# One two-part product for the bias rows, fewer waits and a new order of steps in a two-layer recurrent and attention kernel

## Chip, cores, metric

The kernel runs on one core of a Trainium2 chip. The metric is the device time of one execution in microseconds (us), the median of several runs. The core has five engines with an instruction stream each: PE (TensorE, matrix products), ACT (ScalarE), DVE (VectorE), POOL (GpSimd) and SP (here only the issuer of DMA transfers). Each works through its stream in order; they meet at semaphores.

## What is computed

Two layers on an input of 2 sequences x 2048 tokens x 256 features. In each layer a block's output is multiplied by the SiLU of a second block and added to the input. Cut to what matters here:

```python
# layer 0: a Mamba block, then a gelu MLP; gate: a gated MLP in blockwise FP4
def step(h, inp):
    dt_t, B_t, C_t, x_t = inp
    dA = jnp.exp(dt_t[..., None] * A)          # A: 512 channels x 16 states
    h = dA * h + dt_t[..., None] * B_t[:, None, :] * x_t[..., None]
    y = jnp.sum(h * C_t[:, None, :], axis=-1)
h = jax.nn.silu(fp4_linear(x, w_gate)) * fp4_linear(x, w_up)   # 704 wide
# layer 1: 16-head attention over the 2 sequences; gate: three blocks of
y = _layernorm(_qlora_linear(h, ...)); y = jax.nn.gelu(y); h = _qlora_linear(y, ...) + h
x = x + s * jax.nn.silu(g)
```

The first linear of each of the three blocks, the q and v parts of the attention's input and its output projection have a bias vector of 256 features. Those six are the "bias rows" below.

## The kernel before

**Tiling.** Time is cut into 16 chunks of 128 positions of both sequences (256 tokens, `TOK`). Weights are prepared once (lines 205 to 399: FP4 rounding, transposes, folding of the low-rank parts). Then the five engines run one pipelined loop over `PERIODS` (lines 1276 to 1321).

**The order is written by hand.** Each engine has a list of words, its plan (lines 74 to 106); in a period it runs every word once. A `+` behind a word means the chunk one later than the period's, a `-` one earlier, so one period mixes stages of up to five chunks. A word is a step of `pe_step`, `act_step`, `pool_step`, `dve_step` or `sp_step`, which waits for the semaphores that it needs and then issues its instructions.

**The state engine.** The recurrence runs for 16 states n, each in two halves a and b of the channels. Per state:
- `drive n` (POOL, lines 960 to 972) multiplies `wx` by the state's row of B, then adds eight start values in a second small instruction;
- `exp n` (ACT, line 742) writes the decay into one of three PSUM buffers `unit`, two instructions a half;
- `scan n` (DVE, line 1127) runs the recurrence of a half, `hc n` (line 1133) multiplies it by the row of C, `clr n` (line 1140) clears column 0 of the unit;
- `out n` (ACT, line 750) saves the last column as `carry`. Half k of the chunk uses unit k mod 3, so `exp` of a half waits for the `out` of the half three before it, and that `out` waits for its `clr`;
- `sum n` (PE, line 537) adds it into `y_ps` by transposes; `rows n` (SP) fetches B and C rows from DRAM.

Around it: `dt` and `wx` (DVE) make the chunk's step sizes and `wx`; `log` (POOL) and `dtexp`, `dtln` (ACT) come before `dt`; `arg` (POOL), `first` (ACT) and `fix0`, `fix1` (POOL) make the start values; `yg` (DVE) reads `y_ps` after `sum15`; `fin` (POOL, lines 1068 and 1072) is the last step of a chunk, two tensor operations.

**The banks of PE.** All other products go into three PSUM banks in turn, in the order of `PE_PLAN` without the `sum`s and `skip` (lines 122 to 124). A product waits until the one three places before it has been read by its consumer; `USE` (line 48) names who that is:

```python
BANK = {_key: _k % NBANK for _k, _key in enumerate(ORDER)}
EARLIER = {_key: ORDER[_k - NBANK] for _k, _key in enumerate(ORDER) if _k >= NBANK}
```

The gated MLP is `g00 g01 g10 g11` and `u00 u01 u10 u11` (line 593; first digit: sequence, second: half of the 704 columns). ACT applies SiLU to each g (line 827); DVE's `ug0` multiplies first u00, then u01 into it (two instructions of line 1183), `ug1` does u10 and u11. A g's bank is free after its SiLU, a u's after its multiplication in `ug`. `scale0`, `j0in`, `round0`, `j0out` quantize the product. A bias row is a product (lines 515 to 518) of a one-hot column of `ident` with `b_rows`, in float32.

Of the kernel before, what the change touches and what calls it, by code (L numbers as in the profile page):

```python
# [36 lines left out]
XW = NTAP - 1 + TC  # L37
MAGIC = 1.5 * 2 ** 22
# [42 lines left out]
    exp12a- hq1- hq2- out11a- exp12b- out11b- h1-- exp13a- ctx-- out12a- out12b- exp13b- out13a- exp14a- exp14b-  # L81
    usave dtln gatec--- out13b- exp15a- out14a- exp15b- first out14b- exp0a b1n-- gatem- b1g-- out15a- exp0b
    out15b- s1-- yg0- xq exp1a out0a out0b exp1b yg1- exp2a out1a exp2b g00 out1b g01 exp3a out2a exp3b g10
    out2b g11 exp4a out3a opn- out3b exp4b xn+ xhf+ u2- h2-- exp5a out4a exp5b f10- f11- out4b f12- exp6a out5a
# [11 lines left out]
    hc2a scan2b clr2a hc2b op- clr2b scan3a scan3b h2-- hc3a hc3b clr3a clr3b ug0 scan4a scale0 ug1 hc4a scan4b
    clr4a hc4b scan5a clr4b scan5b hc5a xscale+ hc5b clr5a clr5b round0 scan6a b2s-- hc6a scale1 scan6b clr6a
    hc6b scan7a hc7a clr6b scan7b clr7a hc7b clr7b x1- scan8a conv0+ scan8b hc8a hc8b clr8a conv1+ round1 b0s-
    clr8b scan9a scan9b hc9a hc9b clr9a clr9b scan10a hc10a scan10b clr10a scan11a score- scan11b hc10b hc11a
    clr10b hc11b clr11a attn- clr11b h1- scan12a hc12a scan12b hc12b clr12a clr12b scan13a hc13a clr13a f++  # L100
# [1247 lines left out]
```

## Time and profile before

| | |
|---|---|
| median of 3 runs | 1848.96 us (1847.87 to 1852.0) |
| the profiled execution | 1856.52 us, its span 1854.7 us |
| granted clock of TensorE, mean | 0.953 |
| instructions | 28175 |
| ACT table loads | 109 before `exp` alone, 1283 ns each |
| loop | 16 chunks; first `scan` at 184.5 us, last at 1752.1 us |

The span is the time between the first and the last instruction of the profiled execution; 1.8 us lie outside it. "Busy" is the time in which an engine worked on something; idle time is laid to the engine whose signal ended it. Idle time on an engine that isn't the bottleneck costs nothing. Line numbers stand as L965.

### The profile page before, as it was taken

The numbers are of one execution on the slowest core, as the hardware profiler recorded it, in microseconds if no ns is written. First come the engines' busy times: TensorE is split into PE (matmuls) and PEld (weight loads), VectorE is DVE, ScalarE is ACT, GpSimd is POOL, SyncE is SP. The second block draws the span as 40 slices with busy tenths as digits, with TensorE's granted clock in tenths as the row PEclk, the third lists the DMA queues.
The fourth block names the chain that finished last, engine by engine and source line by source line (L and its number), as shares of the span: only waits on it lengthen the run. The fifth ranks groups of instructions, "written<-read, shape, count | busy, mean of one in ns | idle before, by whom it ended". The sixth has DMA issues, their size and how long they took to land.

```text
span 1854.7 us, 28175 instructions
## 1 busy us (share of the span) xinstructions
PE 1577.4 (85%) x7632; PEld 1164.4 (63%) x7632; DVE 1551.4 (84%) x2882; ACT 1437.5 (78%) x3076; POOL 1252.4 (68%) x1313
## 2 busy tenths in 40 slices
PE   0083768899999999999989999999989999999875
PEld 0051556586767677776767676767667767767653
DVE  0623999999999999999999999999999999999811
ACT  0034678898989898989889888989888989888723
POOL 0304676777777786868687777778686868787522
PEclk9976789999999999999999999999999999999987
DMA  8000111111111111111111111111111211111100
GB/s 209 0 6 29 52 47 58 47 57 37 58 48 60 43 52 51 59 47 52 52 52 52 44 51 50 58 47 46 58 52 47 63 41 58 46 44 55 35 0 12
DMA packets 68395, 91.70 MB, mean 49 GB/s; under 512 B 15674, under 2 KB 34686, under 8 KB 68238
## 3 DMA queue, kind: packets, MB, share of 16 engines
q1 hardware_dynamic: 68238, 89.91, 15.8%
q8 instruction: 62, 1.02, 0.2%
q14 instruction: 95, 0.78, 0.1%
HBM read 85.17 MB, written 4.72 MB: 48 GB/s over the span
## 4 chain that ended last, share of the span: by engine, by line
PE 27%; POOL 20%; DVE 16%; issue 16%; ACT 12%; POOLq 0%; ACTq 0%; DVEq 0%; DMA 0%
PE bank L511 10%; POOL drive L965 10%; PE bank L627 6%; DVE unit L1127 4%; DVE hc L1133 3%; PE bank L516 2%; PE y_ps L537 2%; ACT unit L742 2%; PE bank L498 1%; PE bank L563 1%; ACT op_a L709 1%; DVE xc L1158 1%; ACT L709 1%; ACT L923 1%; POOL s L1068 1%
## 5 line engine op out<-in xcount | busy, mean ns | idle before, releaser
L965 POOL TENSOR_TENSOR drive<-wx,rows 128x1024 f32<-128x1024 f32 x256 | 604.1, 2360 | 163.3 <-DVE unit L1127 82.8
L1127 DVE TENSOR_TENSOR_SCAN unit<-unit,drive 128x512 f32<-128x512 f32 x512 | 616.7, 1221 | 30.7 <-POOL drive L971 23.4
L742 ACT ACTIVATE unit<-dt,aneg 128x254 f32<-128x254 f32 x1024 | 441.9, 468 | 19.8 <-ACT carry L750 0.7
L1133 DVE TENSOR_TENSOR hc<-unit,rows 128x512 f32<-128x512 f32 x512 | 340.9, 684 | 8.8 <-issue 3.0
L537 PE MATMUL y_ps<-ident,hc 128*128 128x128 f32 x2048 | 278.1, 282 | 52.5 <-DVE hc L1133 52.4
L537 PEld LDWEIGHTS y_ps<-ident,hc 128*128 128x128 f32 x2048 | 241.2, 145 | 115.3 <-DVE hc L1133 71.8
L742 ACT ACT_TABLE_LOAD x109 | 139.8, 1283 | 3.7
L750 ACT ACTIVATE carry<-unit 128x4 f32<-128x4 f32 x512 | 79.3, 169 | 66.8 <-DVE unit L1140 63.0
L627 PE MATMUL bank<-op_a,w_f 128*128 128x256 f32 x512 | 115.7, 385 | 11.2 <-ACT op_a L709 11.2
L709 ACT ACT_TABLE_LOAD x77 | 98.8, 1283 | 22.4 <-PE bank L498 21.6
L511 PE MATMUL bank<-w_f,wide 128*128 128x256 f32 x512 | 113.3, 379 | 1.5 <-ACT wide L709 1.5
L627 PEld LDWEIGHTS bank<-op_a,w_f 128*128 128x128 f32 x512 | 97.0, 192 | 27.1 <-ACT op_a L709 11.9
L511 PE MATMUL bank<-w_d,hq_t 128*128 128x256 f32 (+1 forms) x384 | 109.3, 436 | 0.0
L511 PEld LDWEIGHTS bank<-w_f,wide 128*128 128x128 f32 x512 | 96.0, 190 | 14.9 <-ACT wide L709 1.7
L516 PE MATMUL bank<-b_rows,ident 6*128 6x512 f32 (+1 forms) x192 | 100.9, 605 | 0.0
L511 PEld LDWEIGHTS bank<-w_d,hq_t 128*128 128x128 f32 (+1 forms) x384 | 78.6, 219 | 27.0 <-issue 16.4
L593 PE MATMUL bank<-w_g,xq_t 128*128 128x352 f32 x256 | 87.3, 464 | 5.0 <-ACT xq_t L821 5.0
L1013 POOL TENSOR_SCALAR wide<-wx 128x1024 f32<-128x1024 f32 x16 | 58.4, 3652 | 46.8 <-ACT wx L813 46.8
L384 PE MATMUL bank<-ident,gate_raw 88*128 88x88 f32 x32 | 4.9, 355 | 97.2 <-POOL down_raw L314 97.2
L593 PE MATMUL bank<-w_u,xq_t 128*128 128x352 f32 x256 | 84.0, 460 | 1.3 <-ACT hq L827 1.1
L1038 POOL TENSOR_TENSOR hq<-q,j_scl 128x704 f32<-128x704 f32 x32 | 44.4, 1387 | 54.1 <-DVE q L1114 54.1
L722 ACT ACTIVATE xht<-bank,b_sm 128x256 f32<-128x256 f32 x96 | 48.7, 558 | 38.2 <-POOL b_sm L953 38.2
(220 smaller groups left out, 3439.4 us busy)
## 6 DMA issues: line engine op xcount, KB each, us to landing
rows<-rows_scratch SPq DMA_DIRECT2D x256, 256.0 KB, 3.3
x_t<-in_L_attn_x_dram SPq DMA_DIRECT2D x16, 256.0 KB, 3.7
x<-in_L_attn_x_dram SPq DMA_DIRECT2D x16, 256.0 KB, 3.3
out_dram<-x SPq DMA_DIRECT2D x16, 256.0 KB, 2.1
w_f<-in_L_attn_ffn_w_dram SPq DMA_DIRECT2D x2, 1024.0 KB
q_raw<-in_L_ffn_qweights_dram SPq DMA_DIRECT2D x1, 1536.0 KB
w_in<-in_L_attn_in_proj_w_dram SPq DMA_DIRECT2D x1, 1024.0 KB
qkv_raw<-attn_in_proj_weight_dram SPq DMA_DIRECT2D x1, 768.0 KB
```

Source lines behind the costliest of these rows:

```text
L511: last = t.matmul(dst[:, j * D:(j + 1) * D], lhs(k, j), rhs(k), start=(k == 0 and j == 0), stop=(stop and k == kp - 1), skip_group_check=True)
L516: return t.matmul(dst[:, 0:wide_ * D], ident[0:NROW, row:row + 1].to_broadcast([NROW, P]), b_rows[:, None, :].to_broadcast([NROW, wide_, D ...
L537: last = t.matmul(y_ps[j][:, g * P:(g + 1) * P], hc[n % NPROD][:, g * B + j, :], ident[:, :], start=False, stop=(n == NS - 1), is_transpos ...
L593: last = t.matmul(dst[:, 0:IH], xq_t[:, k, j, :], wt[:, k, half * IH:(half + 1) * IH], start=(k == 0), stop=(k == KD - 1))
L627: last = t.matmul(dst[:, a * TOK:(a + 1) * TOK], w_f1[:, k, (2 * m + a) * P:(2 * m + a + 1) * P], op_a[:, k, :], start=(k == 0 and a == 0) ...
L709: last = a_.activation(dst(k), src[:, k * TOK:(k + 1) * TOK], func, scale=scale(k), bias=bias(k))
L742: last = a_.activation(u[:, k * TOK:(k + 1) * TOK].rearrange("p (b t) -> p b t", b=B)[:, :, 1:TC], dt[p][:, g, :].rearrange("p (b t) -> p ...
L750: a_.activation(carry[:, n, 4 * half:4 * half + 4], unit_of(ch, n, half)[:, :].rearrange("p (s t) -> p s t", t=TC)[:, :, TC - 1], ACT.Copy)\
L965: g_.tensor_tensor(drive[n % 2][:, :, :].rearrange("p (g b) t -> p g b t", b=B), wx[p][:, :, :].rearrange("p g (b t) -> p g b t", b=B), ro ...
L1013: g_.tensor_scalar(tmp_u, wx[p][:, :, :], 1.0, -1.0, ALU.add, ALU.add).then_inc(S["sp_pool"], 1)
L1127: v.tensor_tensor_scan(u[:, :], u[:, :], d, 0.0, ALU.mult, ALU.add).then_inc(S["scan_done"], 1)
L1133: v.tensor_tensor(hc[n % NPROD][:, 4 * half:4 * half + 4, :].rearrange("p (g b) t -> p g b t", b=B), unit_of(ch, n, half)[:, :].rearrange( ...
```

## The change

1. **Bias rows.** `b_two` (64 rows of 256, type F32R) holds the bias vectors rounded to F32R in rows 0 to 5 and what the rounding left in rows 32 to 37; one product with the two-hot column `pick` adds both. It takes the place of the float32 product. Four more small loads, one POOL memset and five small DVE operations are added in the preparation.
2. **Waits.** In `exp`, `out`, `drive`, `scan` and `hc`, waits that an earlier wait of the same engine already implies are issued only where they are new.
3. **Order.** All five plans are replaced. Each holds the same words as before.

```diff
 PE_PLAN = """
-    b0a-- xp kv-- sum8- dt0 hqT0- q-- b0T-- sum9- v1-- dt1 b0b-- sum10- hqT1- hqT2- sum11- ctxT-- h1T-- b2b---
-    b1a-- sum12- sum13- dn- sum14- b1T-- sum15- ao-- xqT ygT0- skip ygT1- g00 sum0 g01 op- g10 sum1 g11 b1b--
-    u00 u01 sum2 u10 u2T- u11 sum3 h2T-- f10- f11- f12- f13- b2a-- uT+ sum4 sum5 f2- b2T-- xi0+ xi1+ sum6 z0+
-    sum7 xn1T- xi2+ xi3+ z1+
+    z1 b0a-- sum8- xp kv-- dt0 q-- b0T-- sum9- dt1 hqT0- sum10- v1-- b0b-- sum11- hqT1- h1T-- ctxT-- hqT2-
+    sum12- b1a-- dn- sum13- b2b--- sum14- b1T-- xqT sum15- ao-- ygT0- ygT1- skip sum0 g00 op- b1b-- g01 u00 g10
+    h2T-- g11 u01 sum1 sum2 u2T- u10 u11 f10- sum3 sum4 f11- f12- f13- sum5 b2a-- uT+ f2- b2T-- xi0+ xi1+ sum6
+    z0+ xn1T- xi2+ xi3+ sum7
 """
 ACT_PLAN = """
...
+    exp10b- b0n-- out9b- out10a- exp11a- exp11b- kv-- dt0 out10b- b0g-- aexp-- dt1 v1-- dtexp exp12a- out11a-
+    hq0- exp12b- out11b- exp13a- hq1- h1-- out12a- ctx-- out12b- exp13b- exp14a- dtln out13a- hq2- out13b-
+    exp14b- out14a- exp15a- exp15b- out14b- exp0a b1n-- first gatem- gatec--- b1g-- xq out15a- exp0b out15b-
+    exp1a s1-- out0a yg0- usave out0b yg1- exp1b exp2a out1a exp2b g00 out1b g01 out2a opn- g10 h2-- g11 exp3a
+    out2b exp3b exp4a out3a u2- exp4b out3b xn+ exp5a out4a xhf+ exp5b out4b exp6a f10- f11- f12- out5a out5b
+    f13- exp6b exp7a out6a u+ out6b exp7b out7a b2n-- exp8a exp8b b2g-- tap0+ tap1+ hn- z0+ out7b xn1- tap2+
+    tap3+ xc0+ out8a z1+ xc1+ exp9a exp9b out8b exp10a out9a xp+
 """
 POOL_PLAN = """
-    drive14- drive15- b1-- arg fix0 drive0 xout fin--- drive1 drive2 hb1-- drive3 fix1 f+ drive4 op- drive5 j0in
...
+    drive14- drive15- b1-- arg xout fix0 drive0 fin--- drive1 hb1-- drive2 drive3 op- drive4 f+ drive5 fix1
+    drive6 s0b- drive7 j0in drive8 hb2-- b2-- j0out j1in x1- drive9 hb0- diff- drive10 j1out b0- xin+ drive11
+    drive12 drive13 log+
 """
 DVE_PLAN = """
-    clr15a- xround yg- scan0a clr15b- hc0a scan0b clr0a hc0b clr0b scan1a hc1a clr1a scan1b scan2a hc1b clr1b
...
+    hc15b- wx clr15a- yg- scan0a clr15b- hc0a scan0b clr0a hc0b clr0b scan1a scan1b hc1a clr1a hc1b op- clr1b
+    scan2a hc2a h2-- clr2a scan2b hc2b clr2b ug0 scan3a hc3a scan3b clr3a hc3b clr3b scan4a hc4a scale0 clr4a
+    scan4b scan5a hc4b ug1 clr4b xscale+ scan5b scan6a hc5a clr5a hc5b hc6a clr5b clr6a round0 scan6b hc6b
+    scan7a clr6b b2s-- scan7b hc7a clr7a scale1 hc7b x1- conv0+ scan8a clr7b scan8b hc8a hc8b clr8a clr8b conv1+
+    round1 b0s- scan9a scan9b hc9a scan10a clr9a hc9b scan10b hc10a clr9b clr10a hc10b clr10b scan11a f++ score-
+    scan11b hc11a hc11b clr11a clr11b attn- scan12a h1- scan12b hc12a scan13a clr12a hc12b clr12b hc13a clr13a
+    b1s- scan13b hc13b clr13b scan14a hc14a scan14b clr14a hc14b scan15a dt+ clr14b xround+ hc15a scan15b
 """
...
             def bias_row(dst, row, wide_):
-                return t.matmul(dst[:, 0:wide_ * D], ident[0:NROW, row:row + 1].to_broadcast([NROW, P]),
-                                b_rows[:, None, :].to_broadcast([NROW, wide_, D]), start=False, stop=True,
+                return t.matmul(dst[:, 0:wide_ * D], pick[:, row:row + 1].to_broadcast([2 * LOW, P]),
+                                b_two[:, None, :].to_broadcast([2 * LOW, wide_, D]), start=False, stop=True,
                                 skip_group_check=True)
...
                 u = unit_of(ch, n, half)
-                act.wait_ge(*at("dt_ready", ch))
+                if (n, half) == (0, 0):
+                    act.wait_ge(*at("dt_ready", ch))
...
-                act.wait_ge(*at("carry_in", ch, 1 + n // 8))
+                if n % 8 == 0 and half == 0:
+                    act.wait_ge(*at("carry_in", ch, 1 + n // 8))
...
-                dve.wait_ge(*at("drive_ready", ch, 2 * n + 2))
+                if half == 0:
+                    dve.wait_ge(*at("drive_ready", ch, 2 * n + 2))
...
-                dve.wait_ge(*(at("y_summed", ch, n + 2 - NPROD) if n >= NPROD else at("y_summed", ch - 1, NS + n + 2 - NPROD)))
-                dve.wait_ge(*rows_in(ch, n))
+                if half == 0:
+                    dve.wait_ge(*(at("y_summed", ch, n + 2 - NPROD) if n >= NPROD
+                                  else at("y_summed", ch - 1, NS + n + 2 - NPROD)))
```

The `drive` step's waits for `wx_ready` and `carry_in` are cut in the same way.

## Rows read from the trace of the kernel before

**Rows 1.** The page, part 1: busy time, share of the span, instructions
```profile
PE 1577.4 (85%) x7632; PEld 1164.4 (63%) x7632; DVE 1551.4 (84%) x2882; ACT 1437.5 (78%) x3076; POOL 1252.4 (68%) x1313
```
**Rows 2.** Busy time in one period: start:end, length, busy by engine, granted clock
```profile
863.87:963.53 99.66, 93.36 (x468) 68.95 (x468) 93.98 (x179) 88.89 (x191) 76.86 (x82) 1.00 0.16 52
1063.45:1163.12 99.67, 94.79 (x470) 70.34 (x468) 93.99 (x179) 88.90 (x191) 76.83 (x82) 0.98 0.17 51
```
**Rows 3.** Waits of DVE from 900 to 999.64: total us, times, longest
```profile
DVE unit L1127 <- POOL drive L971: 1.7, 2, 1.3
DVE prod L1224 <- PE bank L516: 0.7, 1, 0.7
DVE s L1205 <- PE bank L529: 0.5, 1, 0.5
DVE xc L1158 <- ACT xc L776: 0.4, 1, 0.4
DVE hc L1133 <- issue: 0.2, 1, 0.2
```
**Rows 4.** Timeline of DVE: start us, us long, instruction, [idle before]
```profile
947.80 0.13 DVE L1140 MEMSET unit<- 128x4 f32 x2
960.09 1.21 DVE L1170 TENSOR_TENSOR wx<-dt,xc 128x1024 f32<-128x1024 f32 x1
965.89 1.28 DVE L1195 TENSOR_TENSOR sz<-y_ps,sz 128x512 f32<-128x512 f32 x2
967.09 1.22 DVE L1127 TENSOR_TENSOR_SCAN unit<-unit,drive 128x512 f32<-128x512 f32 x1
972.32 1.23 DVE L1127 TENSOR_TENSOR_SCAN unit<-unit,drive 128x512 f32<-128x512 f32 x1 [1.29 <-POOL drive L971]
985.84 0.95 DVE L1183 TENSOR_TENSOR hq<-hq,bank 128x352 f32<-128x352 f32 x2
```
**Rows 5.** Timeline of POOL
```profile
943.02 3.65 POOL L1013 TENSOR_SCALAR wide<-wx 128x1024 f32<-128x1024 f32 x1 [1.77 <-ACT wx L813]
961.43 2.35 POOL L965 TENSOR_TENSOR drive<-wx,rows 128x1024 f32<-128x1024 f32 x1
963.86 0.27 POOL L971 TENSOR_TENSOR drive<-drive,fix 128x8 f32<-128x8 f32 x1
967.07 1.26 POOL L1068 TENSOR_TENSOR s<-s,gate_c_sb 128x512 f32<-128x512 f32 x1
989.68 1.39 POOL L1030 TENSOR_TENSOR q<-hq,j_rcp 128x704 f32<-128x704 f32 x1 [0.57 <-DVE j_rcp L202]
```
**Rows 6.** Timeline of PE
```profile
900.89 1.12 PE L516 MATMUL bank<-b_rows,ident 6*128 6x512 f32 x2
919.44 1.15 PE L563 MATMUL bank<-u_t,w_in 128*128 128x262 f32 x4 [0.15 <-ACT sz L788]
983.24 2.53 PE L593 MATMUL bank<-w_u,xq_t 128*128 128x352 f32 x8
```
**Rows 7.** Timeline of ACT
```profile
947.90 0.24 ACT L750 ACTIVATE carry<-unit 128x4 f32<-128x4 f32 x2 [0.31 <-DVE unit L1140]
948.44 0.87 ACT L742 ACTIVATE unit<-dt,aneg 128x254 f32<-128x254 f32 x2 [0.30 <-ACT carry L750]
977.56 0.46 ACT L827 ACTIVATE hq<-bank 128x352 f32<-128x352 f32 x1
978.04 1.28 ACT L742 ACT_TABLE_LOAD   x1
```
**Rows 8.** Waits over the whole span, in the preparation
```profile
DVE q_amax L196 <- DMA lb_raw<-in_L_ffn_lora_b_dram: 45.3, 1, 45.3
DVE unit L1316 <- PEq L287: 34.4, 1, 34.4
```
**Rows 9.** Waits of DVE for ACT over the whole span
```profile
DVE unit L1127 <- ACT unit L742: 4.6, 8, 1.3
```
**Rows 10.** The page, part 6: DMA issues, KB each, us to landing
```profile
rows<-rows_scratch SPq DMA_DIRECT2D x256, 256.0 KB, 3.3
```

More of the change, by code:

```diff
@@ L37 @@
 XW = NTAP - 1 + TC
+LOW = 32
 MAGIC = 1.5 * 2 ** 22
@@ L79 @@
+    h2T-- g11 u01 sum1 sum2 u2T- u10 u11 f10- sum3 sum4 f11- f12- f13- sum5 b2a-- uT+ f2- b2T-- xi0+ xi1+ sum6
+    z0+ xn1T- xi2+ xi3+ sum7
 """
 ACT_PLAN = """
[L81 to L84, printed above, removed]
@@ L85 @@
-    f13- exp6b out5b u+ exp7a b2n-- out6a exp7b out6b exp8a out7a exp8b b2g-- tap0+ tap1+ hn- z0+ xn1- tap2+
-    tap3+ z1+ out7b out8a xc0+ xc1+ exp9a exp9b out8b exp10a b0n- kv- xp+ out9a out9b exp10b exp11a dt0+ out10a
-    exp11b hq0 b0g- aexp- dt1+ out10b v1- dtexp+
+    exp10b- b0n-- out9b- out10a- exp11a- exp11b- kv-- dt0 out10b- b0g-- aexp-- dt1 v1-- dtexp exp12a- out11a-
+    hq0- exp12b- out11b- exp13a- hq1- h1-- out12a- ctx-- out12b- exp13b- exp14a- dtln out13a- hq2- out13b-
+    exp14b- out14a- exp15a- exp15b- out14b- exp0a b1n-- first gatem- gatec--- b1g-- xq out15a- exp0b out15b-
@@ L96 @@
[L96 to L100, printed above, removed]
@@ L102 @@
+    round1 b0s- scan9a scan9b hc9a scan10a clr9a hc9b scan10b hc10a clr9b clr10a hc10b clr10b scan11a f++ score-
+    scan11b hc11a hc11b clr11a clr11b attn- scan12a h1- scan12b hc12a scan13a clr12a hc12b clr12b hc13a clr13a
+    b1s- scan13b hc13b clr13b scan14a hc14a scan14b clr14a hc14b scan15a dt+ clr14b xround+ hc15a scan15b
 """
 SP_PLAN = """
-    rows8- rows11- load+ rows10- rows12- rows13- wr rows14- rows15- rows0 rows1 rows3 rows2 store--- rows4
-    again- rows6 rows5 rows9 rows7
+    rows15-- rows14-- rows0- rows1- rows2- rows3- rows5- rows4- store---- rows7- rows6- rows8- rows10- rows9-
@@ L106 @@
+    again-- rows12- rows11- load+ rows13- wr
 """
@@ L168, in program @@
         w_l = sb("w_l", [P, NLIN, KD, D])
-        b_rows = sb("b_rows", [NROW, D])
+        b_rows = sb("b_rows", [2 * LOW, D])
+        b_two = sb("b_two", [2 * LOW, D], F32R)
+        pick = sb("pick", [2 * LOW, LOW], F32R)
         b_f2 = sb("b_f2", [P, D])
@@ L227, in program @@
                 (w_f2[:, :, :], ffn_w2.rearrange("(k p) n -> p k n", p=P)),
-                (b_rows[0:3, :], biases.rearrange("(i k) d -> i k d", k=2)[:, 0, :]),
-                (b_rows[3:4, :].rearrange("o (h d) -> o h d", d=HD),
-                 qkv_b.rearrange("(h c d) -> c h d", c=3, d=HD)[0:1, :, :]),
-                (b_rows[4:5, :].rearrange("o (h d) -> o h d", d=HD),
-                 qkv_b.rearrange("(h c d) -> c h d", c=3, d=HD)[2:3, :, :]),
-                (b_rows[5:6, :], ao_b[None, :]),
+                *[piece for r in (0, LOW) for piece in (
+                    (b_rows[r:r + 3, :], biases.rearrange("(i k) d -> i k d", k=2)[:, 0, :]),
+                    (b_rows[r + 3:r + 4, :].rearrange("o (h d) -> o h d", d=HD),
+                     qkv_b.rearrange("(h c d) -> c h d", c=3, d=HD)[0:1, :, :]),
+                    (b_rows[r + 4:r + 5, :].rearrange("o (h d) -> o h d", d=HD),
+                     qkv_b.rearrange("(h c d) -> c h d", c=3, d=HD)[2:3, :, :]),
+                    (b_rows[r + 5:r + 6, :], ao_b[None, :]))],
                 (b_l[:, :, :], biases.rearrange("(i k) d -> i k d", k=2)[None, :, 1, :].to_broadcast([P, 3, D])),
@@ L353, in _ @@
                     dve.wait_ge(c_done, 5)
+                    v.tensor_copy(pick[0:LOW, :], ident[0:LOW, 0:LOW]).then_inc(c_prep, 1)
+                    v.tensor_copy(pick[LOW:2 * LOW, :], ident[LOW:2 * LOW, LOW:2 * LOW]).then_inc(c_prep, 1)
+                    dve.wait_ge(c_done, 6)
+                    for r in (0, LOW):
+                        v.tensor_copy(b_two[r:r + NROW, :], b_rows[r:r + NROW, :]).then_inc(c_prep, 1)
+                    dve.wait_ge(c_prep, 6 * len(quants) + 7)
+                    v.tensor_tensor(b_two[LOW:LOW + NROW, :], b_rows[LOW:LOW + NROW, :],
+                                    b_two[LOW:LOW + NROW, :].bitcast(F32), ALU.subtract).then_inc(c_prep, 1)
                     for g in range(DG):
@@ L962, in pool_step @@
                 pool.wait_ge(*rows_in(ch, n))
-                pool.wait_ge(*at("wx_ready", ch))
+                if n == 0:
+                    pool.wait_ge(*at("wx_ready", ch))
                 pool.wait_ge(*at("scan_done", ch, 2 * n - 2))
@@ L969, in pool_step @@
                 pool.wait_ge(*at("drive_ready", ch, 2 * n + 1))
-                pool.wait_ge(*at("carry_in", ch, 1 + n // 8))
+                if n % 8 == 0:
+                    pool.wait_ge(*at("carry_in", ch, 1 + n // 8))
                 g_.tensor_tensor(drive[n % 2][:, :, 0], drive[n % 2][:, :, 0], fix[:, n, :], ALU.add)\
@@ L1296, in _ @@
             def _(act):
-                act.wait_ge(c_done, 7)
-                act.wait_ge(c_prep, 6 * 3 + 3 + DG + NUNIT)
+                act.wait_ge(c_done, 8)
+                act.wait_ge(c_prep, 6 * 3 + 3 + 5 + DG + NUNIT)
                 for c in PERIODS:
@@ L1305, in _ @@
             def _(pe):
-                pe.wait_ge(c_done, 7)
+                pe.wait_ge(c_done, 8)
                 for c in PERIODS:
```

8 lines of the change are left out of this document (3 added, 5 removed).

## The prediction

> **What bounds it now.** I read the shares of busy time first [rows 1]: PE 85% and DVE 84% of the span, but that mixes preparation and loop. So I cut out single periods of the loop by the busy time in windows [rows 2]. One lasts 99.66 us, and in it DVE works 94.0, PE 93.4 to 94.8, ACT 88.9 and POOL 76.9 us. DVE and PE are both nearly full. Then I listed what DVE waits for in one period [rows 3]: 1.7 + 0.7 + 0.5 + 0.4 + 0.2 = 3.5 us. The other 2.1 us of its idle time are gaps of some 30 ns between dependent instructions. So DVE alone would need 99.66 - 3.5 = 96.2 us a period even if nobody ever kept it waiting. That is the floor. The change takes no instruction from DVE in the loop, so it can win at most 3.5 us a period, and it loses whatever new waits its order puts on DVE. All the rest of my work is this count of waits on DVE.
>
> **The bias rows.** There are six a chunk, five of 512 columns and one of 256. One of 512 columns is now two passes over the array that take 1.05 us (1.12 with the tail) [rows 6]. The new one is one instruction. No row shows an F32R product. Its bounds are half of the present pair (0.53 us, if only one of two instructions goes) and a quarter (0.26, if the remaining one also streams twice as fast). I take 0.3. PE gains 5.5 x 0.75 = 4.1 us a period (bounds 2.9 and 4.4). The Trainium skill (FP8 and Floating Point Precision, TensorE Precision Notes) says that true FP32 takes four passes through the array; by it a single pass would be the quarter, 0.26 us; no row here shows a single pass. PE thus needs about 90 of 99.66 us. That relieves it, but DVE's 96.2 stays.
>
> **The waits left out.** On DVE 64 waits a period go (16 before scans, 48 before `hc`), on ACT 61, on POOL about 30. A wait is handled ahead while the engine still works on the instruction before: only 0.2 us a period of DVE's idle time is put down to issue [rows 3]. I take 0.2 us a period; the upper bound is the 2.1 us of small gaps, which I don't believe because the dependent ones remain. A cost below nothing has no reason.
>
> **Table loads on ACT.** Walking the old list I count 19 changes between Exp, Ln, Silu, Gelu and tanh-Gelu a period, in the new one 14. Each costs 1.28 us [rows 7], so ACT gains 6.4 us. The Trainium skill (ScalarE: Activation LUTs, What ACT_TABLE_LOAD costs) puts a load at about 2.7 us, which would make it 13.5 us; the trace has less than half of that. ACT isn't the bound, so this is worth something only where DVE waits for ACT.
>
> **The order.** I walked DVE's new list and asked at each step who releases it, and how much DVE work lies between the releasing and the released step. Five places come out short by construction, wherever the rest of the pipeline stands:
> 1. `wx` to `scan0a`. `drive0` needs `wx`. From the start of `wx` at 960.09 to the end of drive's second instruction at 963.86 + 0.27 is 4.04 us [rows 4, 5], 4.1 with the signal. Before, `scan15b`, two `hc`, `xround` and `yg` lie between. Now only `wx` (1.21, of which the next instruction overlaps 0.09), `clr15a` and `yg` (1.28, likewise) do: 2.4 us. New wait: 1.7.
> 2. `scan1a`. POOL still has `fin` (2 x 1.27) between `drive0` and `drive1` (2.35 + 0.3, as `drive0` [rows 5]): `scan1a` can't start before 5.3 us after `scan0a`, and DVE has 3.9 us of work. This is the 1.29 us of today [rows 4], and stays: 1.3. `xout` moved ahead of `drive0` changes nothing here.
> 3. `ug0`. In the new PE order (`u00 g10 h2T g11 u01`) g11 stands three places behind u00 and takes its bank, and u01 comes after g11. So g11 can't start until `ug0` has multiplied u00, and `ug0`'s second instruction can't start until g11 and then u01 are done. That such bank waits bind is to be seen where xi3 waits for the SiLU of z0, three places before it [rows 6]. Two such products back to back take 2.53 us [rows 6]. With the first multiplication (0.51) and two signals of 0.1 the second starts 3.2 us after the first, against 0.44 now (0.95 for both) [rows 4]. New wait: 2.7. DVE takes its list in order, so nothing fills it.
> 4. `scan3a`. ACT has `g11 exp3a` in this order. From g11's start: product 1.3, SiLU 0.46, table load 1.28, `exp` 0.87 [rows 7] and signals 0.2 make 4.1 us; `ug0` would let DVE go at 2.6 + 0.45 = 3.05. New wait: 1.0.
> 5. `scan10b`. It needs `clr9a`, `out9a`, `exp10b`. From the end of the clears (947.80 + 0.13) to the end of `exp` (948.44 + 0.87) today's fastest case takes 1.4 us [rows 4, 7]; `xp+` (0.3) now sits between. DVE has only `hc9b` (0.7) there. New wait: 0.8 to 1.0; I take 0.8. In the old list every such pair has at least 1.8 us of DVE work between.
>
> Sum: 1.7 + 1.3 + 2.7 + 1.0 + 0.8 = 7.5 us a period, 96.2 - 0.2 + 7.5 = **103.5 us**.
>
> Four more places are short if the other engines stand where I place them when I lay the lists side by side from these durations:
> - `op` on DVE: PE gets to `sum0` before `hc0b` is done and holds g00 and `op` behind it, 0.9 us;
> - `round0`: `j0in` (1.39 [rows 5]) now stands behind `drive7`, which waits for `scan5b`, 1.1 us;
> - `conv0`, now ahead of `scan8a`: ACT puts `exp8b`, a table load and `b2g` before `tap0`, 1.6 us;
> - `scan14a`: `log` (3.65 [rows 5] and two operations of drive's size) still precedes `drive14`; 0.4 to 0.6 us as now.
>
> They add up to 4.2 us, more than half of which hangs on where PE stands, and today's waits for PE at L1224 and L1205 are of the same kind. A wait in one place gives the next engine time to catch up, so I take half: 2.1. The period becomes 105.6 us, bounds 103.5 and 107.7.
>
> SP's list now fetches the rows in swapped pairs (`rows15` before `rows14`, `rows5` before `rows4` and so on). The even one of a pair thus waits for one state's `hc` more, and lands 3.3 us after its issue [rows 10]. The tightest is `drive4`: `rows4` is released by `hc1b` and can be there some 5 us later, when POOL has just done `drive3` and the four small operations of `op`. POOL is idle 22.8 us a period [rows 2], so I take nothing; if that cover is gone, about 1 us, within the bounds.
>
> **Outside the loop.** The four added loads come before the wait of 45.3 us for the last load, a few tenths to 2 us; the five DVE operations lie in a stretch in which DVE afterwards idles 34.4 us [rows 8], nothing. The last chunk has the new waits too, but no full DVE. I take +1.
>
> **Sum.** The loop has 15 full periods. 15 x (105.6 - 99.66) = 89, with +1 it is 90 us: 1856.5 + 90 = 1946.5 for an execution like the profiled one. That one was 7.6 us above the median of the runs shown, so the forecast is **1939 us**. With the bounds 103.5 and 107.7 it is 1908 and 1971; this case's own range is 1905 to 1985.
>
> **Rivals.**
> - *Milder.* The five places are real but shorter, for instance because DVE's 2.1 us of small gaps shrink with its waits and signals are quicker than I took them: a period of 101 to 103.3, 1869 to 1904 us, slower still. For it: the signal times are my estimates. Against: items 2 and 3 rest on measured durations alone.
> - *Faster.* The one mechanism is PE relief without the ring at `ug0` and the early `scan0a`: should my reading of the bank rotation be off, so that u01 is in its bank when `ug0` starts, and `yg` be long enough for `drive0`, then PE's 4.1 us and ACT's 6.4 us remove the waits of today save `scan1a`: 96.2 + 1.3 = 97.5, 15 x -2.2 = -32, 1817 us. It decides from less than 3.3 us of waits left on DVE a period. For it: PE and ACT do get slack, and four of the five waits of today come from them or are near. Against: rows and code of items 1 and 3.
> - *No change.* New waits of just about 3.5 us: 1845 to 1853.
> - *Worse.* PE, held at g11 and at `sum4`, falls behind in the second half and `q`, `b0a` come late: over 108 us a period, above 1985.
> - *The bias product doesn't get shorter.* Then PE needs 94 of 105.6 us; nothing changes in the time, and it is no case of its own.
>
> **Chances.** Forecast 0.68, milder 0.12, worse 0.05, faster 0.12, no change 0.03. The range must leave out no more than 2 in 10: forecast and milder together are 0.80, 1865 to 1985. A measurement of this kernel tells a difference from about 0.2%. Slower by more than that: 0.68 + 0.12 + 0.05 = 0.85; within: 0.03; faster: 0.12.
>
> **What would show it.** In the trace of the changed kernel: in each period a wait of 2.7 us of DVE L1183 for PE L593; `scan0a` and `scan1a` waiting 1.7 and 1.3 us for POOL L971; waits of DVE L1127 for ACT L742 of about 1 us twice a period (4.6 us in the whole span now [rows 9] would become over 25); 14 table loads a period; PE busy about 90 us a period; a period of 104 to 107 us. Wrong if L1183 never waits, or if DVE's busy time itself changed. If the five waits are there and the period is still under 101 us, my floor is wrong.

## The result, and the profile after

| | before | changed |
|---|---|---|
| median, 4 runs each | 1849.46 us (1847.87 to 1852.0) | 2082.4 us (2081.7 to 2089.97) |
| ratio, with its 95% interval | 1 | 1.1267 (1.1238 to 1.1297) |
| profiled execution, its span | 1856.52, 1854.7 us | 2089.97, 2088.2 us |
| period of the loop, mean of ten | 99.72 us | 115.42 us |
| DVE kept waiting, per period | 3.55 us | 16.73 us |
| granted clock of TensorE, mean | 0.953 | 0.927 |

The change costs 233 us. The forecast was 1939 us with a range of 1865 to 1985: the sign was right and the size was not, by 143 us. Fifteen periods of 115.4 instead of the forecast 105.6 us make 147, about as much, so the error lies in the loop.

In the changed kernel the numbers of the lines are some 13 to 19 higher: scan is L1145, hc L1152, clr L1159, out L765, exp L756, drive L981 and L988, ug L1202, the bias product L529.

The page of the changed kernel, part 1 (to hold against [rows 1]) and two lines of part 5 (costliest groups; busy us, mean ns of one, idle before it and its releaser):

```profile
PE 1606.4 (77%) x7536; PEld 1190.0 (57%) x7536; DVE 1583.3 (76%) x2887; ACT 1339.3 (64%) x2999; POOL 1228.7 (59%) x1314
...
L1145 DVE TENSOR_TENSOR_SCAN unit<-unit,drive 128x512 f32<-128x512 f32 x512 | 618.7, 1222 | 112.1 <-ACT unit L756 69.0
...
L765 ACT ACTIVATE carry<-unit 128x4 f32<-128x4 f32 x512 | 85.5, 172 | 375.9 <-DVE unit L1159 374.7
```

All shares fell. DVE's busy time rose by 32 us, with five more instructions, and PE's rose by 29 us although 96 instructions are gone. The scan waits for 112 us in the whole span, and 69.0 of them end at an `exp` of ACT, where it was 4.6 [rows 9].

Next, one period: its length, busy time by engine (PE, PEld, DVE, ACT, POOL), granted clock. It answers to [rows 2]:

```profile
999.66:1115.15 115.49, 96.34 (x465) 71.31 (x464) 96.12 (x179) 82.68 (x185) 75.15 (x82) 0.96 0.14 44
```

DVE executes the same 179 instructions in 96.1 us that took it 94.0. Then the waits of DVE in the same period (total us, times, longest), which answer to [rows 3]:

```profile
DVE unit L1145 <- ACT unit L756: 4.0, 6, 1.0
DVE hq L1202 <- PE bank L606: 2.7, 1, 2.7
DVE unit L1145 <- POOL drive L988: 2.7, 2, 1.5
DVE b_st L1100 <- PE bank L529: 2.4, 1, 2.4
DVE prod L1243 <- PE bank L529: 2.0, 1, 2.0
DVE q L1124 <- POOL q L1047: 1.0, 1, 1.0
DVE sd L1252 <- ACT sd L938: 0.9, 1, 0.9
DVE s L1218 <- PE bank L524: 0.8, 1, 0.8
DVE xc L1177 <- ACT xc L791: 0.4, 1, 0.4
...
```

To see which step each of them is, I went down DVE's timeline of that period with the new list beside it (start, us, instruction, in brackets the wait; the instructions between these are left out):

```profile
1000.37 0.84 DVE L201 TENSOR_SCALAR x_scl<-x_amax 128x32 f32<-128x32 f32 x1
...
1007.11 0.53 DVE L1124 TENSOR_SCALAR q<-q 128x704 int32<-128x704 int32 x1 [1.00 <-POOL q L1047]
...
1046.94 0.69 DVE L1243 TENSOR_TENSOR prod<-bank,kv 128x512 f32<-128x512 f32 x1 [1.98 <-PE bank L529]
1055.54 1.23 DVE L1145 TENSOR_TENSOR_SCAN unit<-unit,drive 128x512 f32<-128x512 f32 x1 [1.01 <-ACT unit L756]
1064.15 0.76 DVE L1100 BATCH_NORM_STATS2 b_st<-bank 128x6 f32<-128x256 f32 x2 [2.39 <-PE bank L529]
1083.25 1.23 DVE L1145 TENSOR_TENSOR_SCAN unit<-unit,drive 128x512 f32<-128x512 f32 x1 [1.47 <-POOL drive L988]
1088.42 2.35 DVE L1145 TENSOR_TENSOR_SCAN unit<-unit,drive 128x512 f32<-128x512 f32 x2 [1.21 <-POOL drive L988]
1092.90 0.69 DVE L1218 TENSOR_TENSOR s<-bank,xn 128x512 f32<-128x512 f32 x1 [0.82 <-PE bank L524]
1102.37 0.52 DVE L1202 TENSOR_TENSOR hq<-hq,bank 128x352 f32<-128x352 f32 x1 [2.73 <-PE bank L606]
1103.94 1.23 DVE L1145 TENSOR_TENSOR_SCAN unit<-unit,drive 128x512 f32<-128x512 f32 x1 [1.04 <-ACT unit L756]
```

In this order these are `x_scl`, `round0`, `score`, `scan12a`, `b1s`, `scan0a`, `scan1a`, `op`, `ug0`, `scan3a`. The ones that I had priced are there at nearly their prices. `score` and `b1s`, 4.4 us together, stand nowhere in my sum.

On the other side of the units, ACT's waits for `clr` in the same period:

```profile
ACT carry L765 <- DVE unit L1159: 21.4, 15, 2.9
```

and in one period of the kernel before:

```profile
ACT carry L750 <- DVE unit L1140: 2.3, 4, 1.1
```

ACT now stands at its `out`s for 21.4 us in this period, and what comes behind them in its list stands with them.

### The profile page after: what moved, and what is told of

Same layout as the page of the kernel before. It is cut to its first block, busy times and chain, and to the rows that moved or that the text cites. A ratio compares the mean times of both kernels' runs of the same rounds, so it can differ in the third digit from the quotient of the medians.

```text
span 2088.2 us, 26204 instructions
## 1 busy us (share of the span) xinstructions
PE 1606.4 (77%) x7536; PEld 1190.0 (57%) x7536; DVE 1583.3 (76%) x2887; ACT 1339.3 (64%) x2999; POOL 1228.7 (59%) x1314
## 4 chain that ended last, share of the span: by engine, by line
DVE 36%; PE 18%; issue 17%; ACT 14%; POOL 9%; POOLq 0%; DVEq 0%; ACTq 0%; DMA 0%
DVE unit L1145 13%; PE bank L524 7%; DVE hc L1152 7%; POOL drive L981 5%; ACT unit L756 4%; PE bank L606 2%; PE y_ps L550 2%; DVE xc L1177 2%; ACT L756 2%; PE bank L640 2%; DVE q L1129 2%; ACT xht L735 1%; DVE q L1127 1%; DVE b_st L1100 1%; PE bank L594 1%
## 5 line engine op out<-in xcount | busy, mean ns | idle before, releaser
L981 POOL TENSOR_TENSOR drive<-wx,rows 128x1024 f32<-128x1024 f32 x256 | 603.8, 2359 | 387.7 <-DVE unit L1145 350.5
L1145 DVE TENSOR_TENSOR_SCAN unit<-unit,drive 128x512 f32<-128x512 f32 x512 | 618.7, 1222 | 112.1 <-ACT unit L756 69.0
L756 ACT ACTIVATE unit<-dt,aneg 128x254 f32<-128x254 f32 x1024 | 434.9, 467 | 11.3 <-DVE dt L1185 6.3
L550 PE MATMUL y_ps<-ident,hc 128*128 128x128 f32 x2048 | 282.3, 285 | 118.4 <-DVE hc L1152 117.3
L1152 DVE TENSOR_TENSOR hc<-unit,rows 128x512 f32<-128x512 f32 x512 | 345.6, 683 | 7.4
L765 ACT ACTIVATE carry<-unit 128x4 f32<-128x4 f32 x512 | 85.5, 172 | 375.9 <-DVE unit L1159 374.7
L640 PE MATMUL bank<-op_a,w_f 128*128 128x256 f32 x512 | 139.0, 433 | 21.6 <-ACT op_a L722 21.6
L640 PEld LDWEIGHTS bank<-op_a,w_f 128*128 128x128 f32 x512 | 110.9, 222 | 48.2 <-ACT op_a L722 28.4
L722 ACT ACT_TABLE_LOAD x62 | 79.5, 1283 | 36.8 <-PE bank L511 36.0
L606 PE MATMUL bank<-w_g,xq_t 128*128 128x352 f32 x256 | 92.6, 487 | 11.0 <-DVE hq L1202 8.7
L756 ACT ACT_TABLE_LOAD x78 | 100.1, 1283 | 1.4
L1100 DVE BATCH_NORM_STATS2 b_st<-bank 128x6 f32<-128x256 f32 x96 | 36.3, 420 | 71.0 <-PE bank L529 71.0
L576 PE MATMUL bank<-u_t,w_in 128*128 128x262 f32 x256 | 75.8, 427 | 16.9 <-DVE s L1224 5.8
L594 PE MATMUL bank<-xps,w_dt 16*128 16x256 f32 x128 | 45.3, 485 | 49.6 <-ACT xht L735 44.0
```

The source lines that it names most:

```text
L550: last = t.matmul(y_ps[j][:, g * P:(g + 1) * P], hc[n % NPROD][:, g * B + j, :], ident[:, :], start=False, stop=(n == NS - 1), is_transpos ...
L576: last = t.matmul(dst[:, 0:B * XW], w_in[:, k, g * P:(g + 1) * P], u_t[:, k, :, :], start=(k == 0), stop=(k == KD - 1))
L594: last = t.matmul(dst[:, a * TOK:(a + 1) * TOK], w_dt[32:48, (2 * m + a) * P:(2 * m + a + 1) * P], xps[32:48, :], start=(a == 0), stop=Tru ...
L606: last = t.matmul(dst[:, 0:IH], xq_t[:, k, j, :], wt[:, k, half * IH:(half + 1) * IH], start=(k == 0), stop=(k == KD - 1))
L640: last = t.matmul(dst[:, a * TOK:(a + 1) * TOK], w_f1[:, k, (2 * m + a) * P:(2 * m + a + 1) * P], op_a[:, k, :], start=(k == 0 and a == 0) ...
L722: last = a_.activation(dst(k), src[:, k * TOK:(k + 1) * TOK], func, scale=scale(k), bias=bias(k))
```

## Experiments

"Period" is the mean of ten full periods of the one profiled execution, and waits are DVE's per period in the same ten. Ratios are to the kernel before on the same chip. The runs come from several chips, so edits of the changed kernel are held against its ratio of 1.1267 (1.1238 to 1.1297) and its period of 115.42, and not against its microseconds.

**Which of the three parts costs the time.** First the changed kernel with the five old lists in place of the new ones:

```diff
-PE_PLAN, ACT_PLAN, POOL_PLAN, DVE_PLAN, SP_PLAN = (the new lists)
+PE_PLAN, ACT_PLAN, POOL_PLAN, DVE_PLAN, SP_PLAN = (the old lists)
```

> The changed kernel with the five old plans: bias product in two parts and fewer waits, old order. Theory A (the new order puts waits on DVE, and that is the whole loss): between the kernel before and 1.5% faster, 1822 to 1850 us, PE busy about 91 us a period instead of 94. Theory B (the two-part product or the missing waits are at fault, the order only in part): slower than before by several per cent, over 1900 us.

Measured: 1839.34 us, ratio 0.9923 (0.9895 to 0.9952), period 98.97, waits 2.82 us. It is faster than both kernels, within the range of theory A. Its waits from 900 to 998.97:

```profile
DVE unit L1145 <- POOL drive L988: 1.8, 2, 1.3
DVE xc L1177 <- ACT xc L791: 0.4, 1, 0.4
```

Against [rows 3] the waits of 0.7 and 0.5 us for PE are gone (in the mean of ten 0.3 and 0.1 are left), and the bias product, half as long, stands ahead of the first of them. PE is busy 91.8 us a period instead of 94.4 (both means of ten).

The second is the kernel before with the wait edits alone (the last diff block of the change, and the same in `drive`):

> The kernel before with only the implied waits left out. Theory A: waits are handled ahead of the engine, 1845 to 1853 us. A rival, that each wait left out saves DVE the 20 to 50 ns of its record: 64 a period, 1.3 to 3.2 us a period, 1800 to 1830 us.

Measured: 1847.39 us, 0.9981 (0.996 to 1.0003). No difference that can be told from none. My 0.2 us a period is neither shown nor excluded by the times. The trace speaks against it: the period is 99.75 against 99.72, and the wait at `hc` that was laid to issue, 0.22 us a period before, is still there with 0.28, now laid to PE's `y_ps`. The rival of 1.3 us a period and more is excluded.

The third is the kernel before with the five new lists alone, the float32 bias rows and all waits kept:

> The kernel before with only the five new plans: float32 bias product, all waits. Theory A: as slow as the changed kernel or a little slower, 2080 to 2130 us (PE gets 3 us a period more work, but it isn't what DVE waits for most). Theory B: clearly faster than the changed kernel, under 2000 us.

Measured: 2139.6 us, 1.1531 (1.1475 to 1.1588), period 118.45, waits 19.52. The order alone costs more than the whole change, and a little more than theory A had for it. The other two parts give 0.8% back on the old lists and 2.3% on the new ones (1.1267 over 1.1531). There DVE waits behind bias products: with the long ones `b1s` waits 2.99 us and `score` 2.62, against 2.40 and 1.78 in the changed kernel. That is half of the 2.8 us by which its waits are longer; the granted clock is lower too (0.904 against 0.927), and no run parts the two.

**Taking the named waits away, one at a time.** Each is a move of one or two words in the changed kernel.

`wx` ahead of the period's end, against items 1 and 2 of my working:

```diff
 DVE_PLAN
-    hc15b- wx clr15a- yg- ...   dt+ clr14b xround+
+    hc15b- clr15a- yg- ...      dt+ clr14b wx+ xround+
```

> The changed kernel with wx for the next chunk before xround on DVE. Additive: scan0a's wait of 1.3 to 1.5 us gone, 2060 us. Rival: scan0a still waits, now for the start values (arg, first, fix0), because POOL's xout stands before fix0 and waits for xround: under 0.5 us a period, above 2073 us.

Measured: 2086.27 us, 1.1257 (1.1189 to 1.1325), period 115.39. Both waits for `drive` went (0.09 us left of 2.5), and the time didn't move. The size is the rival's, its reason isn't: `scan0a` doesn't wait for the start values. Two lines of its waits from 1000 to 1115.4 tell why:

```profile
DVE s L1218 <- PE bank L524: 2.4, 1, 2.4
DVE sz L1214 <- PE y_ps L550: 1.7, 1, 1.7
```

`yg` (L1214, just ahead of `scan0a`) and `op` (L1218) wait for PE, whose chain (`sum15`, `ygT`, `skip`, `sum0`, `g00`, `op`) runs beside `drive0` and ends nearly as late. The wait changed its name.

The bank ring at `ug0` opened, with ACT's list shifted to suit:

```diff
 PE_PLAN
-    g01 u00 g10 h2T-- g11 u01 sum1
+    g01 u00 u01 g10 h2T-- g11 sum1
 ACT_PLAN
-    opn- g10 h2-- g11 exp3a out2b exp3b exp4a
+    opn- exp3a out2b g10 h2-- exp3b g11 exp4a
```

> The changed kernel with u01 before g10 on PE, exp3a before g10 and exp3b before g11 on ACT. If the wait of 2.73 us at the second multiplication of ug0 and the 1.04 us at scan3a are additive: 3.8 us a period less, about 2025 us. If ACT's lateness takes their place (new waits of scan for exp): under 1.5 us a period, above 2060 us. Two more table loads a period on ACT, 2.6 us.

Measured: 2100.27 us, 1.1332 (1.1265 to 1.14), period 116.10. The 2.7 us at L1202 are gone, so the reading of the ring is right. Its waits from 1000 to 1116.1 show where they went:

```profile
DVE unit L1145 <- POOL drive L988: 4.6, 3, 1.9
DVE unit L1145 <- ACT unit L756: 5.2, 7, 1.9
```

The edit isn't a clean removal: it puts four more table loads a period into ACT's list (18 in the trace where there were 14, 5.1 us), and not the two that I had expected. A part of the 5.2 us is its own doing.

`b1s` three steps later on DVE:

```diff
 DVE_PLAN
-    hc13a clr13a b1s- scan13b hc13b clr13b scan14a
+    hc13a clr13a scan13b hc13b clr13b b1s- scan14a
```

> The changed kernel with b1s two steps later on DVE, behind clr13b. DVE has 2.0 us more work before it. Additive: 2.0 to 2.4 us a period less, 2045 to 2052 us. Rival: POOL's b1 root, b1n and b1T on the way to sum15 come late and yg waits instead: no gain.

Measured: 2071.14 us, 1.1175 (1.1102 to 1.1249), period 114.02. The wait of 2.4 us went, waits for `drive` grew by 0.9, and 1.4 us a period are won, which is between the two expectations. The interval of the ratio just touches that of the changed kernel, so the gain rests on the periods of two traces.

All four moves of this kind together (these three, and `b0n` of the next group):

> The changed kernel with four places mended: wx for the next chunk right behind clr14b; u01 before g10 on PE with exp3a before g10 on ACT; b0n ahead of out9a and xp on ACT; b1s behind clr13b on DVE. Theory A, waits add up: about 1.5 + 3.8 + 4 + 2.4 = 11.7 us a period less, 115.5 to 104, 1905 to 1930 us. Rival, each place mended uncovers the next engine's lateness: half of it, 1980 to 2010 us.

Measured: 2051.77 us, 1.1086 (1.1039 to 1.1133), period 112.81. 6.9 us of waits at `ug0`, `b1s` and `score` went, and the period gave 2.6, less than either expectation. This kernel too has the four more table loads. From 1000 to 1112.8 there are instead, beside others:

```profile
DVE unit L1145 <- ACT unit L756: 5.4, 9, 1.9
DVE s L1218 <- PE bank L524: 1.6, 1, 1.6
```

So waits don't add up: where named ones are taken away, others appear. `wx_early` shows it with no more work on any engine.

**Why `score` waits for `q`.** PE's timeline in the changed kernel, and beside it the granted clock in stretches of 2 us (the third number from the end of each line):

```profile
1035.55 1.98 PE L695 MATMUL bank<-w_qkv,xd 128*128 128x512 f32 x4
1040.68 1.79 PE L594 MATMUL bank<-xps,w_dt 16*128 16x256 f32 x4 [3.15 <-ACT xht L735]
1042.40 3.78 PE L524 MATMUL bank<-w_qkv,op_b 128*128 128x256 f32 x8
1046.11 0.79 PE L529 MATMUL bank<-b_two,pick 64*128 64x512 f32 x1
```

```profile
1036.00:1038.00 2.00, 1.53 (x4) 0.38 (x2) 2.00 (x3) 0.00 (x0) 1.92 (x4) 1.00 0.00 0
1038.00:1040.00 2.00, 0.00 (x0) 0.00 (x0) 1.29 (x4) 1.54 (x5) 1.92 (x2) 1.00 0.00 0
1040.00:1042.00 2.00, 1.32 (x4) 0.94 (x4) 1.99 (x5) 0.99 (x5) 0.96 (x2) 0.75 0.52 146
1042.00:1044.00 2.00, 2.00 (x6) 1.33 (x5) 1.51 (x4) 2.00 (x6) 1.66 (x2) 0.50 0.03 9
...
1048.00:1050.00 2.00, 2.00 (x14) 1.44 (x13) 1.97 (x5) 1.96 (x3) 0.07 (x1) 1.00 0.00 0
```

`dt0` takes the bank of `b0a`, and that is free when ACT has done `b0n`, which now stands behind `exp10b`. PE waits 3.15 us, and at 1041.0, 0.3 us after it has gone on, the granted clock goes from 1.00 to 0.50 (2.4 to 1.2 GHz) for 6.8 us. The products of `dt0`, `q` and the bias run slowly: `q` takes 3.78 us. The Trainium skill (TensorE: Matmul & The Clock Gate, HAM oscillation — how this bites in real kernels) describes a PE that is kept waiting and starts its next burst at the lower clock; the trace agrees but for those 0.3 us.

To part the clock from the wait, I let the product `kv` ahead of it be made twice. The result is the same, and PE has 1.9 us more to do:

```diff
-                for k in range(KD):
+                for k in 2 * [*range(KD)]:
                     last = t.matmul(dst[:, :], xd[:, k, :], w_qkv[:, k, D:3 * D], start=(k == 0), stop=(k == KD - 1))
```

> The changed kernel with the kv product made twice in a row into the same bank (same result, 1.9 us more work for PE), which covers most of PE's 3.15 us of idle time before dt0. If PE's fall to half clock after that idle time is what makes q long: the clock stays at 1.0, q back to 1.9 us, DVE's wait for q (1.8 us) mostly gone, 1 to 1.8 us a period less although PE does more work, 2055 to 2070 us. If the clock isn't tied to the idle time: q stays at 3.8 us and the time doesn't fall.

Measured: 2067.73 us, 1.1153 (1.1105 to 1.12), period 113.58: more work, and 1.8 us a period less. Its timeline of PE:

```profile
1032.94 3.70 PE L695 MATMUL bank<-w_qkv,xd 128*128 128x512 f32 x8
1038.07 1.12 PE L594 MATMUL bank<-xps,w_dt 16*128 16x256 f32 x4 [1.43 <-ACT xht L735]
1039.12 1.99 PE L524 MATMUL bank<-w_qkv,op_b 128*128 128x256 f32 x8
```

A part of the idle time was filled, the clock held, `q` takes 1.99 us and `score` waits for nothing. `dt0` still waits for its bank. Within this one kernel the comparison comes again: in 10 of the 14 periods in which `dt0` comes right behind `kv` and is kept waiting the clock held, `q` took 1.99 us and `score` waited 0.14 us at most; in the other four it fell behind the same 1.43 us of idle time, `q` took 2.69 to 3.68 us and `score` waited up to 0.91. So it is the slow clock behind this wait that makes `score` late.

The other remedy is to free the bank earlier, by `b0n` ahead of the period's last `out`:

```diff
 ACT_PLAN
-    exp10b- b0n-- out9b-     ...     exp10a out9a xp+
+    exp10b- out9b-           ...     exp10a b0n- out9a xp+
```

> The changed kernel with b0n right behind exp10a on ACT, so that the bank of b0a is free before dt0. Expected: PE's wait of 3.15 us at dt0 gone, the q product back from 3.8 to 1.9 us because PE's granted clock doesn't fall, score's wait of 1.8 us gone, scan10b's wait longer (ACT does 1 us more before exp10b): net 1 to 2.5 us a period less, 2045 to 2065 us. If the long q product has nothing to do with the wait ahead of it, it stays at 3.8 us and score still waits.

Measured: 2098.64 us, 1.1324 (1.1284 to 1.1363), period 115.27. The expectation failed: `dt0` still waits 1.55 us, now for `xps`, and the clock still falls. `q` takes 2.79, and `score`'s wait is gone, but 1.96 us for v at `ctx` took its place. The slow clock now lasts 13.7 us at this place (1055.4 to 1069.0) and falls on the product for v, which takes 1.91 us instead of 1.03.

The two moves that gained, together (`b1s` late, `kv` twice):

> The changed kernel with both edits that gained alone: b1s behind clr13b, and the kv product made twice. If they are independent: 115.4 - 1.4 - 1.8 = 112.2 us a period, 2030 to 2040 us. If they cover each other: 2055 to 2068 us, as the better one alone.

Measured: 2050.23 us, 1.1053 (1.1 to 1.1106), period 112.63. 2.8 us of the 3.2 that the two gave singly: these two nearly add up. The time lies between the two expected ranges.

**The scans that wait for ACT.** Item 5 blamed `xp` between `out9a` and `exp10b`. Moved behind:

```diff
 ACT_PLAN
-    exp10b- b0n--       ...     exp10a out9a xp+
+    exp10b- xp b0n--    ...     exp10a out9a
```

> The changed kernel with xp behind exp10b on ACT, not before it. scan10b's wait of 0.7 us should go; PE's dt0 already waits for b0n behind it on ACT, so dt0 isn't later. If that gain stands: 0.5 to 0.8 us a period less, 2070 to 2076 us. If ACT is in any case held by out9b and out10a right behind: within 0.3 us a period, 2077 to 2088 us.

Measured: 2092.79 us, 1.1287 (1.1205 to 1.1368), period 115.30. Waits for `exp` fell by 0.36 us of 4.1, that of `score` grew by 0.3, and no difference in the time can be told from none. So `xp` ahead of `exp10b` isn't worth its 0.7 us.

**Whether POOL's and SP's new lists cost the time.** Old lists for POOL and SP, new ones for the other three:

```diff
-POOL_PLAN, SP_PLAN = (the new lists)
+POOL_PLAN, SP_PLAN = (the old lists)
```

> The changed kernel with the old lists of POOL and SP; the new ones of PE, ACT and DVE stay. If the loss is in those three, as the waits say: within 1.5% of the changed kernel, 2060 to 2110 us. If POOL's or SP's list has a part of it: under 2040 us.

Measured: 2256.66 us, 1.2172 (1.2136 to 1.2207), period 126.30. Its waits from 1000 to 1120:

```profile
DVE hq L1202 <- PE bank L606: 7.2, 1, 7.2
DVE sz L1214 <- PE y_ps L550: 6.7, 1, 6.7
```

Slower by far, outside both expectations. It says only that the new lists of POOL and SP together suit the other new lists better than the old ones do. No run exchanges the list of PE, ACT or DVE singly. SP's swapped pairs cost POOL no wait, as I had taken it: in the whole span POOL waits 2.6 us for rows from DRAM in the changed kernel, and 80.2 before.

**DVE's own instructions.** `x_scl` in the timeline above takes 0.84 us. POOL's timeline shows what ran beside it and beside `j_scl`:

```profile
999.91 1.26 POOL L1064 TENSOR_TENSOR s<-s,b_f 128x512 f32<-128x512 f32 x1
...
1016.65 1.39 POOL L1055 TENSOR_TENSOR hq<-q,j_scl 128x704 f32<-128x704 f32 x1
```

`x_scl` ends at 1001.21, 40 ns after POOL's L1064; `j_scl` lasts from 1016.95 to 1018.08, 40 ns beyond L1055. The kernel with POOL's `s0b` moved away:

```diff
 POOL_PLAN
-    drive6 s0b- drive7 j0in drive8 hb2--
+    drive6 drive7 j0in drive8 s0b- hb2--
```

> The changed kernel with POOL's s0b (1.27 us) moved from before drive7 to after drive8, away from DVE's xscale. If the long small DVE instruction there (x_scl, 0.85 us instead of 0.18) is held by the POOL instruction that runs: it takes 0.18 us again, round0's wait for j0in (1.0 us) goes too; up to 1.7 us a period less, 2057 to 2075 us. If it is long for another reason it stays at 0.85 us.

Measured: 2097.09 us, 1.1311 (1.1239 to 1.1383), period 116.17. All instructions of the two kinds, changed kernel first, then this one (ns, shortest/median/longest):

```profile
L201 DVE TENSOR_SCALAR j_scl<-j_amax x32: 185/187/1142, 198.1 to 1939.3; 128x44 f32<-128x44 f32 x32
L201 DVE TENSOR_SCALAR x_scl<-x_amax x16: 180/850/1049, 135.2 to 1808.7; 128x32 f32<-128x32 f32 x16
```

```profile
L201 DVE TENSOR_SCALAR j_scl<-j_amax x32: 186/186/189, 208.7 to 1959.7; 128x44 f32<-128x44 f32 x32
L201 DVE TENSOR_SCALAR x_scl<-x_amax x16: 181/181/181, 145.8 to 1826.8; 128x32 f32<-128x32 f32 x16
```

The held time is gone and DVE works 1.5 us less a period. The time isn't less, against the expectation: `round0` still waits, and with `s0b` moved something else is late:

```profile
DVE xc L1177 <- ACT xc L791: 2.6, 1, 2.6
```

(its waits from 1000 to 1116.2). The cause of the long instructions is shown; what they cost in time isn't.

**The one wait left on the old lists.** There, where `scan1a` waits 1.3 us for `drive1` behind `fin`, I exchanged the two:

```diff
 POOL_PLAN (old)
-    drive0 xout fin--- drive1 drive2
+    drive0 xout drive1 fin--- drive2
```

> The changed kernel with the five old lists and fin moved behind drive1 on POOL. If scan1a's wait of 1.3 us is worth its full length: 98.97 to 97.7 us a period, 1815 to 1825 us. If the engines behind take its place, as in the four single repairs: 1830 to 1845 us, no difference to the old order.

Measured: 1888.5 us, 1.0199 (1.0168 to 1.023), period 102.75, 3.8 more than the same kernel without the exchange. From 900 to 1002.75:

```profile
DVE unit L1145 <- ACT unit L756: 3.8, 1, 3.8
```

The wait for POOL fell to 0.53 us. But ACT's `s1` waits for `fin`, and stands ahead of the next `exp`s in ACT's list: a later `fin` holds ACT, and ACT holds the scan for three times as long (its own wait at `s1` is 3.8 us, and 1.2 without the exchange). Both expectations failed.

## Why the prediction was wrong in size

**Right: the sign, and the sizes of what was named.** The five places by construction, predicted and measured in the period shown: `scan0a` 1.7 and 1.47, `scan1a` 1.3 and 1.21, `ug0` 2.7 and 2.73, `scan3a` 1.0 and 1.04, `scan10b` 0.8 and 0.71. Sum 7.5 and 7.16. Of the four soft ones `op` came with 0.82 (0.9), `round0` with 1.00 (1.1), `conv0` with 0.36 (1.6) and `scan14a` with nothing: 2.18, and I had taken 2.1. That this sum fits is luck: I had halved it because a wait gives the next engine time to catch up, and what came is two places whole, one at a quarter and one not at all. Together 9.34 us for 9.6. Table loads fell from 19 to 14 a period, 1283 ns each. The 2.7 us that I quoted from the Trainium skill (ScalarE: Activation LUTs, What ACT_TABLE_LOAD costs) is by that section a load of 1283 ns and a drain; the load agrees, and no such drain shows: ACT idles some 18 ns before a load and 12 behind it. That the kernel becomes slower by a wait in nearly every stage, though ACT works 6 us less a period (82.7 for 88.9), held too. That each of these waits is worth its length isn't borne out: two of them gone gave nothing in `wx_early`.

**Failed: "five places come out short by construction".** The count wasn't complete. In the period shown the other waits are 7.7 us:
- `b1s` 2.39. By my own rule it was a sixth: `b1a` and its bias row stand behind `sum12` on PE, which waits for `hc12b`, and DVE has only `clr12b hc13a clr13a` before `b1s`, some 0.8 us. PE's part:

```profile
1060.87 1.09 PE L550 MATMUL y_ps<-ident,hc 128*128 128x128 f32 x8 [1.86 <-DVE hc L1152]
1061.80 1.89 PE L524 MATMUL bank<-w_l,op_b 128*128 128x256 f32 x8
1063.62 0.49 PE L529 MATMUL bank<-b_two,pick 64*128 64x512 f32 x1
```

  From 1060.87 to 1064.11 are 3.2 us. I had asked what makes the banks of DVE's inputs at the gated MLP, and not here. `b1s_late` took this wait away.
- `score` 1.98, by the clock. The bank of `dt0` and the place of `b0n` stand in the lists, and I never asked what a PE that stands does to the products behind. `kv_twice` shows it.
- attention 1.1 (`attn` 0.94 and `ctx` 0.15, for ACT), `scan11a`, `scan12a`, `scan14b` and `scan15a` 2.3 in all, each for an `exp`. Over the span the scans wait 69.0 us for `exp`, where I had written "over 25".

**Failed: "DVE would need 96.2 us even if nobody ever kept it waiting".** In the changed kernel the period less the waits is 98.7 us (means of ten here). DVE is busy 96.4 us instead of 94.0, with the same instructions. 1.6 us of that are `x_scl` and `j_scl`, held beside POOL; in `s0b_late`, where none is held, DVE is busy 1.5 us less. Most of the rest is overlap: DVE mostly starts an instruction some 0.08 us before the last one ends, but not behind a wait. There are 16 waits in the period shown instead of 6, and the overlaps sum to 7.4 us a period instead of 8.0. The prediction had named a changed busy time as its sign of error, and had not looked at what runs beside what when POOL's steps move, though the trace of the kernel before shows held instructions (last section).

The account for the period shown: 96.0 forecast floor, + 9.3 named places, + 7.7 unnamed, + 2.4 longer floor make 115.4, against 115.49. It has to add up, since the last term is what the period has left over. It says where the time lies, and not what each wait would give back.

**The bias product** was taken at 0.3 us and takes 0.49 at full clock, near my upper bound of 0.53. PE's relief on the old lists is 2.7 us a period and not 4.1. In the changed kernel it works 96.3 us in the period instead of 90, of which the slow clock has its part. By the Trainium skill (FP8 and Floating Point Precision, TensorE Precision Notes) I had estimated 0.26 us for a single pass; the measurement decides.

**The rivals.** "Worse" had a chance of 0.05, over 1985 us, and the time came out there. It had named that `q` comes late, and `q` did, but its mechanism isn't what came: PE doesn't fall behind at g11, it stands at `dt0` and then runs slowly, and that is 2.0 us of the 7.7. The chance was far too small: all that I hadn't looked at pointed to this side, for an unlisted wait can only be added to the sum. "Milder" needed a period of at most 103.3 us. "Faster" and "no change" needed 3.5 us of waits or less; there are 16.7.

**What stays open.** The 4.1 us a period of waits for `exp` weren't isolated by a run: that ACT is held at `out` by DVE, and so gives each unit late, rests on the 21.4 us and the order of the list and is argued. In `ring_off` and `all_four` the new names of the waits show where the time went, but no run says how much of it was the 5.1 us of table loads that these edits brought along. Nor is it known what the held instructions cost in time, or which of the three lists of PE, ACT and DVE has what part.

## What to carry over

- With in-order queues, go down the whole new list of the engine that bounds, step by step, and compute for each step releaser, path and cover; a place that isn't on the list isn't at zero. If only a part has been walked, the range must be open on the slow side.
- A wait that is taken away is worth what the next latest path leaves of it: here 2.5 us of waits for `drive` gave nothing, 2.4 us at `b1s` gave 1.4, and exchanging two steps on POOL to save a wait of 1.3 us cost 3.8. Look at who else reads the moved step, on every engine.
- Test the parts of a change apart: two of the three here make a kernel that is 0.8% faster, beneath an order that alone costs 15%.
